# Cross-attention of a two-block perceiver: inverse roots taken for four batches at once, the two half-products summed by the output projection, the last key's value folded in there too

## The reference

```python
q = heads(query @ Wq + bq); k = heads(key @ Wk + bk); v = heads(value @ Wv + bv)   # block 0
scores = q k^T / sqrt(16) + mask * -1e9;  out = softmax(scores) v;  return out @ Wo + bo
q = rms_norm(x @ Wq.T, q_norm_w); k = rms_norm(context @ Wk.T, k_norm_w)           # block 1
q, k = rope(q), rope(k);  out = softmax(q k^T / 4) (context @ Wv.T);  return out @ Wo.T
```

## Time and profile before

| | |
|---|---|
| median of 3 runs | 1277.69 us (1276.63 to 1279.93) |
| the profiled execution | 1276.58 us, of which its span is 1274.7 us |
| PE / PE weight loads busy | 996.5 us (78%) / 794.9 us (62%) |
| DVE busy | 607.9 us (48%) |
| ACT busy | 494.9 us (39%) |
| POOL busy | 335.0 us (26%) |
| mean granted TensorE clock | 0.888 of full speed |

### The profile page before, as it was taken

One profiled execution on the slowest core, in us unless ns is written; L12 is line 12 of the kernel. 1 busy time (PEld: TensorE's weight loads), 2 busy tenths in 40 slices (PEclk: granted clock), 3 DMA queues, 4 the chain that ended last, 5 costly groups with the idle time before them and its releaser, 6 DMA issues.

```text
span 1274.7 us, 24294 instructions
## 1 busy us (share of the span) xinstructions
PE 996.5 (78%) x8506; PEld 794.9 (62%) x8506; DVE 607.9 (48%) x1835; ACT 494.9 (39%) x1442; POOL 335.0 (26%) x494
## 2 busy tenths in 40 slices
PE   5999999888873899998147888888768875199990
PEld 3677667544652799997135656565548764199980
DVE  4555666513634011112775888888744554022222
ACT  3665666533330333322134555555545652011100
POOL 3111120002104000003527776777602100400004
PEclk9899999988985899999578999999986776599995
DMA  8111124000004788883100001100000000679953
GB/s 247 35 35 35 61 82 149 2 1 0 1 1 190 260 336 316 330 325 120 29 33 18 30 24 35 34 33 1 2 1 1 1 0 1 225 288 334 329 214 100
DMA packets 50562, 135.75 MB, mean 106 GB/s; under 512 B 16168, under 2 KB 37552, under 8 KB 44464
## 3 DMA queue, kind: packets, MB, share of 16 engines
q1 hardware_dynamic: 47408, 126.28, 27.8%
q0 software_dynamic: 3072, 8.39, 2.0%
HBM read 117.36 MB, written 17.30 MB: 106 GB/s over the span
## 4 chain that ended last, share of the span: by engine, by line
PE 60%; DVE 22%; issue 7%; ACT 3%; POOL 3%; SPq 2%; DMA 2%; DVEq 0%; another core or an unknown queue 0%; POOLq 0%; ACTq 0%
PE lower L1091 13%; PE upper L1100 9%; PE upper L649 6%; PE upper L617 5%; PE upper L850 3%; PE upper L685 3%; PE lower L671 2%; POOL xslot L2144 2%; PE upper L702 2%; PE lower L831 2%; PE upper L931 2%; DVE arena L1552 2%; PE upper L719 2%; DVE x L1960 1%; PE lower L566 1%
## 5 line engine op out<-in xcount | busy, mean ns | idle before, releaser
L1091 PEld LDWEIGHTS lower<-arena 128*128 128x128 f32 x1472 | 175.0, 195 | 6.1 <-DVE arena L1926 3.9
L1091 PE MATMUL lower<-arena 128*128 128x128 f32 x1472 | 176.0, 279 | 2.6 <-DVE arena L1926 2.6
L649 PE MATMUL upper<-wkv,arena 128*128 128x256 f32 x512 | 140.4, 398 | 12.0 <-ACT arena L1192 6.8
L1100 PE MATMUL upper<-arena 128*128 128x256 f32 x552 | 126.4, 379 | 0.0
L2150 POOL DMA_INDIRECT arena<-yslot,slot x32 | 30.7, 958 | 323.5 <-DMA yslot<-arena 314.3
L649 PEld LDWEIGHTS upper<-wkv,arena 128*128 128x128 f32 x512 | 90.5, 192 | 34.6 <-issue 12.3
L1100 PEld LDWEIGHTS upper<-arena 128*128 128x128 f32 x552 | 101.5, 190 | 12.0
L1450 ACT ACTIVATE arena<-lower,arena 128x128 f32<-128x128 f32 x184 | 52.5, 369 | 106.3 <-PE lower L1091 106.3
L1217 ACT ACTIVATE arena<-lower,arena 128x257 f32<-128x257 f32 x128 | 59.6, 474 | 60.2 <-DVE arena L1530 60.2
L2034 POOL TENSOR_TENSOR arena<-arena 128x512 f32<-128x512 f32 x64 | 70.6, 1114 | 36.4 <-ACT klast L1270 20.7
L685 PE MATMUL upper<-const,arena 128*128 128x128 f32 x512 | 77.8, 275 | 1.7 <-ACT arena L1227 1.4
(11 more groups left out here) (236 smaller groups left out, 1885.1 us busy)
## 6 DMA issues: line engine op xcount, KB each, us to landing
arena<-in_ew_dram SPq DMA_DIRECT2D x23, 2048.0 KB, 7.2
arena<-in_ew_dram SPq DMA_DIRECT2D x23, 1536.0 KB, 6.1
arena<-in_ctxT_dram SPq DMA_DIRECT2D x16, 1028.0 KB, 5.1
xslot<-zero SPq DMA_DIRECT2D x2, 2944.0 KB, 15.4
arena<-xslot SPq DMA_DIRECT2D x46, 128.0 KB, 5.9
yslot<-arena SPq DMA_DIRECT2D x46, 128.0 KB, 6.2
const<-in_const_dram SPq DMA_DIRECT2D x1, 1154.0 KB, 7.6
x<-in_x_dram SPq DMA_DIRECT2D x1, 1024.0 KB, 5.7
```

Source lines behind the costliest of these rows:

```text
L649: ins = mm(bank[6 + w][:, 0:D], dctx[k2][:, c, j2, w * P:w * P + P], wkv[l][:, c, D:2 * D], start=(c == 0), stop=(c == KC - 1))
L1091: ins = mm(bank[1 + half][:, i * P:i * P + P], ew[k][:, at:at + P], exT[k % 2][:, c, :], start=(c == 0), stop=(c == KC - 1))
L1100: ins = mm(bank[4 + k % 2][:, 0:D], eh[k % 2][:, i, :], ew[k][:, at:at + D], start=(i == 0), stop=(i == nh - 1))
```

## The change

`merge` becomes one vector instruction: both half-products times 1/sum go to `attended`, which doubles. `output` multiplies each half with Wo, four matmuls instead of two, and a fifth with 4 rows adds Wo applied to the last key's value (`vwo`, and in block 0 the output bias), spread over the tokens by a constant. `vwo` is made once per block by 16 matmuls (`last_outputs`) and four copies. The addition of the bias to x goes. In block 0 TensorE's `last_values` now waits for the same DMAs as the mask. The inverse roots are taken for four batches at once, sums 7 slots ahead and keys 8 ahead in block 1. GpSimd's rotation takes both halves of the keys in four instructions. TensorE's `project` moves behind the first half of `keys`; VectorE's `merge` moves behind `shares` and `maxima`, and `added` behind `turned`. `weigh` stays between the two halves of `values`.

```diff
+        vwo = sb("vwo", [QB, NT, D])
...
-        KEYS_AHEAD = (2, 6)
-        DIFF_AHEAD = (2, 5)
-        SUMS_AHEAD, NORM_AHEAD, ROPE_AHEAD, TURN_AHEAD = 5, 4, 3, 2
+        KEYS_AHEAD = (2, 8)
+        DIFF_AHEAD = (2, 7)
+        SUMS_AHEAD, NORM_AHEAD, ROPE_AHEAD, TURN_AHEAD = 7, 4, 3, 2
...
                 def last_values():
 
-                    pe.wait_ge(lastkeys_loaded, 16 * KC)
+                    pe.wait_ge(mask_loaded, 16 * (QB + 1 + KC))
...
+                def last_outputs():
+
+                    for b in range(4):
+                        for t in range(2):
+                            n = 2 * b + t
+                            for c in range(KC):
+                                ins = mm(bank[b][0:QB, t * D:t * D + D], vlast[l][:, c, QB * n:QB * n + QB], wo[l][:, c, :],
+                                         start=(c == 0), stop=(c == KC - 1))
+                        ins.then_inc(q["lastvals"], 1)
...
-                    pe.wait_ge(q["krope"], KW2 * b2 + w + 1)
+                    pe.wait_ge(q["krope"], b2 + 1)
...
+                    if isinstance(b2, int) and b2 == 0:
+                        pe.wait_ge(q["vwc"], 4)
...
                     for c in range(KC):
-                        ins = mm(bank[5][:, 0:D], attended[k][:, c, :], wo[l][:, c, :], start=(c == 0), stop=(c == KC - 1))
-                    ins.then_inc(q["ow"], 1)
+                        for e in range(2):
+                            mm(bank[5][:, 0:D], attended[k][:, c, e, :], wo[l][:, c, :], start=(c == 0 and e == 0), stop=False)
+                    mm(bank[5][:, 0:D], const[0:QB, C_TOKB:C_TOKB + P], vwo.rearrange("j n d -> j (n d)")[:, bass.ds(n * D, D)],
+                       start=False, stop=True).then_inc(q["ow"], 1)
...
                 def slot(n, k, j, it):
                     turns(n, k, j, it, 0)
                     scores(n, k, j, it)
+                    keys(n, k, j, it, 0)
                     if there(n):
                         project(n, k, j)
-                    keys(n, k, j, it, 0)
...
                 elif early:
                     pe.wait_ge(wx_loaded[l], 48)
                     last_values()
                     last_keys()
-                    pe.wait_ge(q["lvc"], 1)
+                    pe.wait_ge(q["lastvals"], 2)
...
                     turn_last_keys()
+                    last_outputs()
                     slots(pe, slot, 1 - EARLY, -1)
                     pe.wait_ge(q["qrope"], 1)
+                    pe.wait_ge(q["vwc"], 4)
...
                     act.wait_ge(q["lastkeys"], 6)
+                    for b in range(4):
+                        act.wait_ge(q["lastvals"], b + 3)
+                        A(vwo[:, 2 * b:2 * b + 2, :], bank[b][0:QB, :].rearrange("j (n d) -> j n d", d=D), copy)\
+                            .then_inc(q["vwc"], 1)
                     A(klast[:, :, :], bank[5][:, 0:KC * B].rearrange("p (c b) -> p c b", c=KC), copy).then_inc(q["lastkeys"], 1)
...
-                    V.tensor_tensor(pairs.rearrange("p c e q -> p (c e q)"), bank[5][:, 0:P], parts_of, ALU.mult)\
-                     .then_inc(q["merge"], 1)
-                    dve.wait_ge(q["merge"], 2 * b + 1)
-                    V.tensor_tensor(merged, pairs[:, :, 0, :], pairs[:, :, 1, :], ALU.add).then_inc(q["merge"], 1)
-                    dve.wait_ge(q["merge"], 2 * b + 2)
-                    V.tensor_tensor(attended[k][:, :, T * j:T * j + T], merged,
-                                    vlast[l][:, :, bass.ds(b, 1)].to_broadcast([P, KC, T]), ALU.add).then_inc(q["outc"], 1)
+                    V.tensor_tensor(attended[k][:, :, :, T * j:T * j + T],
+                                    bank[5][:, 0:P].rearrange("p (c e q) -> p c e q", c=KC, e=2),
+                                    parts_of.rearrange("p (c e q) -> p c e q", c=KC, e=2), ALU.mult).then_inc(q["outc"], 1)
...
-                        if half:
+                        if j2 == QB - 1:
...
-                            inv_root(flat(kr), flat(kss), 2 * KW2 * NH, rooted)
+                            inv_root(flat(kr), flat(kss), QB * KW2 * NH, rooted)
...
                     n0, k0, j0, _ = ahead(n, k, j, it, -1)
+                    shares(n, k, j, it)
+                    maxima(n, k, j, it)
                     if there(n0):
                         merge(n0, k0, j0)
-                    shares(n, k, j, it)
+                    keys(n, k, j, it, 0)
+                    turned(n, k, j, it)
                     if j == 1 and there(n) and not (isinstance(n, int) and n == 0):
                         added(n - 1)
-                    maxima(n, k, j, it)
-                    keys(n, k, j, it, 0)
-                    turned(n, k, j, it)
                     keys(n, k, j, it, 1)
...
-                    for t in range(NT):
-                        ins = V.tensor_tensor(x[:, t, :], x[:, t, :], bo_bc[:, :], ALU.add)
-                    mine(ins)
+                    for b in range(4):
+                        dve.wait_ge(q["lastvals"], b + 3)
+                        V.tensor_tensor(vwo[:, 2 * b:2 * b + 2, :], bank[b][0:QB, :].rearrange("j (n d) -> j n d", d=D),
+                                        bo_bc[0:QB, :].unsqueeze(1).to_broadcast([QB, 2, D]), ALU.add).then_inc(q["vwc"], 1)
...
-                    for w in range(KW2):
-
-                        after(pool, q["krope"], KW2 * b2 + w)
-                        rope(krope[j2 % 2][:, w, :], kn[j2 % 2][:, w, :], P, rope_k(w), "krope", KW2 * b2 + w + 1)
+
+                    after(pool, q["krope"], b2)
+                    rope(krope[j2 % 2], kn[j2 % 2], P, 0, KW2, "krope", b2 + 1)
```

78 lines of the change are left out of this document (37 added, 41 removed).

## The result

The changed kernel takes 1303.2 us (median of 4 runs, 1300.8 to 1306.1) against 1277.2 us for the kernel before beside it: 2.1% slower, ratio 1.0206 with a 95% interval of 1.0172 to 1.024. The forecast was 1316, with a range of 1289 to 1331.

A forecast was written before the change was run, and what follows sets the result against it. TensorE was taken to bound the first loop, with both engines near their end in the second. Terms 17.5 + 1 + 4 - 1 + 16 + 2 = 39.5 on 1276.6 gave 1316 us, range 1289 to 1331.

The forecast's parts named there:

- the main term: First loop, seven projection slots: TensorE waits for `merge` behind the maxima and runs five matmuls, +17.5 us.
- one term of 16: Second loop: the root slot and the later projection lengthen each row tile by a net 2.3 us, +16 in all.
- Projection in the first loop: Seven slots: 1.4 us of idle for `merge`, five matmuls and shape changes add 2.5 per slot, +17.5 us.
- `merge` in the other slots: Slots without projection: its 0.29 us delays the copy `weigh` needs where that copy is already last, +1 us.
- Start: First block: last values wait for later DMAs, then `last_outputs` takes 7.4 us; first maxima at 36.5, +4 us.
- Second block before its loop: Two more batches and wider roots cost 3 us; a root leaving slot -2 and the rotation give 4 back, -1.
- Second loop: Per tile, projection at s + 12.6 and next scores 21.7 after the root slot's; other slots 0.9 shorter; +16 us.
- Last projections: Outside the loops: three more matmuls, 1.4 us, less 0.4 for fewer `merge` steps, twice, +2 us.
- half of the wait: TensorE's projection idle is partly paid back as others catch up; second loop breaks even, 1297 us; chance 0.17.
- Changes of shape drain TensorE: Around the projection's 4-row matmul both switches cost 0.39 us, adding 8: 1324 us; chance 0.10.
- `added` starves the key copies: Second loop: second key copy waits behind `added`, TensorE loses 1.2 us more per tile, 1330 us; chance 0.09.
- VectorE's relief decides: VectorE's 4.5 us less work per tile shortens the second loop by 31.5, 1261 us; chance 0.07.

The follow-up runs named there:

- experiment 1: Place of `merge`: changed kernel with `merge` ahead of shares and maxima, 1269.4 us; kernel before with `merge` and the addition behind the maxima, 1365.0 us.
- halves alone: The changed kernel with roots over two batches again, keys 6 and sums 5 ahead, rotation still in four instructions: 1300.4 us, ratio 1.0192.

## Why the prediction was right, and where its steps failed

The direction and the main term held. The sum was 39.5 against 26 by the medians and 28 by the profiled spans, because one term of 16 did not come and two small ones were too small. That these misses partly offset each other is luck: the second loop with its last projection was put 17 too high, the start and the stretch before the second loop 9 too low, and 4 us came off in stretches that nobody had priced.

- *Projection in the first loop, +17.5, and the last one's share.* Right. The idle was 1.17 to 1.34 us for 1.4, the slot 10.1 to 10.26 for 10.0, the seven slots together 17.5 longer, and the whole loop 20.2 for the 17.5 + 1 + 1 of the terms in it. Moving `merge` took 13.9 of it away, so it was the wait; the fifth matmul costs 0.77 a time where I had 0.46 and 0.2.
- *`merge` in the other slots, +1.* Quiet slots kept their 6.15 us; some beside GpSimd's burst went from 7.21 to 7.40. Right for one instruction. That the kernel before with `merge` and `added` in this place lost 92 us shows how narrow it was; how much of that is the number of steps is not separated (experiment 1).
- *Start, +4.* 6.4. The working was right at full clock: the kernel with halves alone, whose start has the same code, had its first maxima at 36.46 for the 36.5 forecast. In the changed kernel they were at 38.24, as the clock fell and `last_outputs` took 8.8 us for the 7.4 assumed. The shared semaphore, for which I had charged 2.2, measured 2.3, and the 1.7 of the clock went with it; I had no term for the clock.
- *Second block before its loop, -1.* It was +5.8. The root left slot -2 as foreseen, but the query chain gave 2.2 back for the 4 that I had taken for it and the rotation. What failed is "up to +3.8; part of it can fall into idle time, and I take 3": it was 8.0. Every kernel with roots over four batches has an early stretch of 51 to 52 us, every one with two batches 43.3 to 44.2, so it is the two extra batches. I had counted what VectorE does for a batch. A batch has its matmuls, ACT's part and GpSimd's differences too; which of them fills the 8 us I did not separate.
- *Second loop, +16.* It was -0.3: the step that failed. Scaling came at s + 8.05 for s + 9.6, the projection at s + 10.6 for 12.6, and the next scores 19.35 behind the root slot's for 21.7; the other two slots were right (14.36 for 14.9). I had added 0.8 for the wider root steps to the 8.53 of before. But VectorE before the change, in order of time in that slot,

```profile
822.70 0.89 DVE L1630 TENSOR_SCALAR root_v<-arena 128x64 f32<-128x64 f32 x1
823.62 0.66 DVE L1631 TENSOR_SCALAR root_y<-root_v 128x64 int32<-128x64 int32 x1
824.32 0.19 DVE L1632 TENSOR_SCALAR root_y<-root_y 128x64 int32<-128x64 int32 x1
```

  and GpSimd beside it,

```profile
822.50 1.04 POOL L2034 TENSOR_TENSOR arena<-arena 128x512 f32<-128x512 f32 x1
...
823.62 0.62 POOL L2040 TENSOR_TENSOR arena<-qT,const 128x256 f32<-128x256 f32 x1
```

  had two steps that stood still until GpSimd was done (0.20 for the same step alone). In the changed kernel GpSimd is through when the roots start, and these steps, twice as wide, take 0.23 each. The rest of the miss is the length of what follows: I let VectorE do shares in 0.53, a mean with the blocked ones in it, and it took 0.29.
- *Last projections, +2.* From the last scores to the transposes behind the block it was 22.6 us for 20.1 in the first block, and 15.5 for 15.3 in the second: 2.8 together, nearly all in the first block and there part of the 20.2.

Of the rivals, *half of the wait* (1297) was nearest: in time the result lies between it and the forecast. Its second loop, which breaks even, came true. Its reason, that the others catch up meanwhile, is at most a small part: from the projection to the next scores it was 8.7 us for the 9.1 forecast, 0.4 per tile of some 3; most came before the projection. *Changes of shape drain TensorE* was partly true, at 0.15 each. *`added` starves the key copies* showed once per tile, with 0.92 us of wait at `turn_keys`, but not as a lengthening. *VectorE's relief decides* I had given 0.07 with the condition that `merge` be done before TensorE has issued the first keys. The condition was the right one: with `merge` moved there the kernel took 1269 for that rival's 1261.

What I missed altogether is that the gain was there and was hidden by one instruction's place.

## What to carry to other kernels

Where a change shortens a step and also moves it, price the place on its own: ask who waits for the step and for everything queued behind it, and try the old place with the new step. A mean duration that is well above the lone one (0.53 against 0.29 here) can be a wait inside the row, which goes or grows when the other engine is shifted: look whether the row ends with one of the other engine. Putting GpSimd's work into wider instructions saves its own time and lengthens what VectorE may stand still for; which of the two counts depends on who is late in that slot. Before a row's length is put down to the instruction, read the granted clock beside it: 16 matmuls took 7.07 or 8.76 us by the clock alone.

## What was not expected of the hardware

- VectorE's instructions with two on-chip operands, and its `tensor_scalar` too, ran until the GpSimd instruction beside them ended: 0.23 became 1.29 us, and in the first loop with `merge` first a `tensor_scalar` of 0.17 became 0.70 and 0.85. Reciprocals and reductions of one operand, and instructions with one in PSUM, kept their time in those rows. It goes the other way as well: GpSimd's 512-wide step took 3.31 us instead of 1.27 while VectorE worked through the long instructions of the query chain.
- Two engines that trigger each other can lock into a slower rhythm: slots of 9.03 us, one like the other, where 7.11 was possible; the same work in narrower pieces broke it (41 us in the loop).
- An idle time of 2.12 us in TensorE was followed by a granted clock of 0.85 and 0.73 in the stretches of 8 us from 752 and 760 us, and the slot took 14.94 us, where it took 10.35 without the idle time. Equal idle times did not always do this: after 1.76 us the clock stayed at 1.00 and after 1.74 us it fell to 0.82, in the same kernel.
- A matmul with 4 rows between two of full shape cost 0.77 us for 0.46, while 16 matmuls onto 4 rows, one behind the other, took 0.44 each at full clock.
